# First feed-forward of a four-layer kernel: the last tile of the inner dimension stacked, gate on up and high part on low part

## What is computed

```
gate = einsum('bsh,oh->bso', x, lut[gate_idx])      # gate_idx, up_idx: 688 x 256
up   = einsum('bsh,oh->bso', x, lut[up_idx])
h    = silu(gate) * up                              # inner dimension 688
out  = einsum('bsh,oh->bso', h, lut[down_idx])      # down_idx: 256 x 688
```

## Time and profile before

| | |
|---|---|
| median of 3 runs | 2064.55 us (2063.49 to 2067.57) |
| profiled execution | 2068.32 us, span 2066.5 us |
| granted TensorE clock, mean of the span | 0.952 of full speed |
| PE busy | 1837.7 us, 89% of the span, 13335 instructions |
| PEld busy | 1266.3 us, 61% |
| DVE busy | 1374.8 us, 67%, 3587 instructions |
| ACT busy | 740.8 us, 36% |
| POOL busy | 901.9 us, 44%, 965 instructions |
| chain that ended last, by engine | PE 68%, DVE 19%, issue 6%, POOL 2%, ACT 2% |
| largest line of the chain | PE L1029, 16% |

### The profile page before, as it was taken

The page is one execution under the profiler, slowest core; times in us unless marked ns, Lnnn a source line. Parts: engine busy times, 40 slices in busy tenths (PEclk is TensorE's granted clock), DMA queues, the critical chain, the costliest instruction groups (busy, mean ns, idle before and its releaser), DMA issues.

```text
span 2066.5 us, 39950 instructions
## 1 busy us (share of the span) xinstructions
PE 1837.7 (89%) x13335; PEld 1266.3 (61%) x13400; DVE 1374.8 (67%) x3587; ACT 740.8 (36%) x1511; POOL 901.9 (44%) x965
## 2 busy tenths in 40 slices
PE   8999999689997899999999988899867788998887
PEld 5555555489996455555555446677655667885443
DVE  4677767465554656565656567888846776886775
ACT  2544444122222464656464541111122223443332
POOL 0354545465555254545454443333343224663333
PEclk9999999799999899999999999999999888999787
DMA  5300000100004646454545400000011000000011
GB/s 181 106 6 8 5 8 6 35 6 10 9 10 95 138 84 112 84 109 81 109 81 111 79 7 14 8 10 8 15 32 41 13 16 16 16 13 18 31 38 41
DMA packets 68177, 93.34 MB, mean 45 GB/s; under 512 B 9852, under 2 KB 62316, under 8 KB 64748
## 3 DMA queue, kind: packets, MB, share of 16 engines
q1 hardware_dynamic: 68076, 92.01, 19.6%
HBM read 61.70 MB, written 29.49 MB: 44 GB/s over the span
## 4 chain that ended last, share of the span: by engine, by line
PE 68%; DVE 19%; issue 6%; POOL 2%; ACT 2%; DMA 1%; DVEq 1%; SPq 0%; POOLq 0%; ACTq 0%
PE PS L1029 16%; PE PS L2084 3%; PE PS L677 3%; DVE negmax L2322 3%; PE PS L1960 3%; PE PS L1196 3%; PE PS L734 3%; PE PS L750 2%; PE PS L510 2%; PE PS L2012 2%; DVE xn L500 2%; PE PS L2015 2%; PE PS L731 2%; PE PS L2057 2%; PE PS L701 1%
## 5 line engine op out<-in xcount | busy, mean ns | idle before, releaser
L2322 DVE TENSOR_REDUCE negmax<-PS 128x2 f32<-128x512 f32 (+1 forms) x384 | 247.1, 685 | 191.6 <-PE PS L2015 98.0
L541 POOL TENSOR_TENSOR X<-X,y_sb 128x512 f32 (+1 forms) x128 | 165.2, 1291 | 147.7 <-DVE y_sb L536 142.7
L536 DVE TENSOR_TENSOR y_sb<-PS,ga_sb 128x512 f32<-128x512 f32 x96 | 66.2, 690 | 180.3 <-PE PS L1029 50.4
L1029 PE MATMUL PS<-we_hi,h_parts 128*128 128x512 f32 x512 | 177.7, 407 | 1.6 <-POOL h_parts L1478 1.5
L500 DVE TENSOR_SCALAR xn<-X,mv,rs 128x256 f32 (+1 forms) x256 | 155.6, 649 | 22.5 <-POOL rs L493 21.2
L520 ACT ACTIVATE hT<-PS,modT 128x256 f32<-128x256 f32 x256 | 130.0, 559 | 112.5 <-PE PS L510 111.6
L2237 ACT ACTIVATE pw<-PS 128x512 f32<-128x512 f32 x256 | 139.0, 600 | 75.0 <-PE PS L2060 75.0
L491 POOL TENSOR_TENSOR rs<-mv,eps 128x2 f32<-128x2 f32 x128 | 26.6, 208 | 293.4 <-DVE mv L484 293.2
L1029 PE MATMUL PS<-l_h_parts,lut_hi 128*128 128x256 f32 (+1 forms) x768 | 145.7, 291 | 6.7 <-POOL l_h_parts L1162 6.7
L1029 PEld LDWEIGHTS PS<-l_h_parts,lut_hi 128*128 128x128 f32 (+1 forms) x768 | 117.8, 184 | 9.7 <-issue 5.4
L1572 DVE SCALAR_TENSOR_TENSOR l_acc<-PS,rt_g,l_acc 128x256 f32<-128x256 f32 x256 | 105.8, 475 | 20.8 <-PE PS L1029 20.7
(11 more groups left out here) (279 smaller groups left out, 4372.3 us busy)
## 6 DMA issues: line engine op xcount, KB each, us to landing
ga_sb<-ga_dram SPq DMA_DIRECT2D x128, 128.0 KB, 2.9
qk_dram<-qk_parts SPq DMA_DIRECT2D x64, 192.0 KB, 2.8
KS<-qk_dram SPq DMA_DIRECT2D x32, 384.0 KB, 5.9
QS<-qk_dram SPq DMA_DIRECT2D x32, 384.0 KB, 9.3
qk_dram<-qk_parts SPq DMA_DIRECT2D x64, 128.0 KB, 2.8
wmod<-in_wmod SPq DMA_DIRECT2D x4, 1536.0 KB, 13.6
qk_dram<-qk_parts SPq DMA_DIRECT2D x64, 64.0 KB, 2.5
y_out<-X SPq DMA_DIRECT2D x16, 256.0 KB, 2.2
```

The source lines that it names most:

```text
L541: pool.tensor_tensor(xb(b), xb(b), y_sb[b.par][:, :, :], ALU.add).then_inc(s.x.sem, 1)
L1029: last_ = pe.matmul(out, x.bitcast(F32R), y.bitcast(F32R), start=start and n == 0, stop=stop and n == 2)
L2322: dve.tensor_reduce(to, src, AX.X, ALU.max, negate=True).then_inc(s.max.sem, 1)
```

## The change

The tiles of the inner dimension become 4 of 128, one of 112 and one of 64 (TAIL) rows. The index layout puts the last 64 columns of up directly behind gate, so that the last 64 columns of gate and of up are one weight tile of 128 columns: its product has gate on PSUM partitions 0 to 63 and up on 64 to 127. ACT writes the silu to partitions 64 to 127, DVE multiplies there and writes `hid` to partitions 0 to 63. The rows of the last tile of down stand twice, on partitions 0 to 63 and 64 to 127. The low part of the last hidden tile is made by DVE, no longer by POOL, and written to partitions 64 to 127 under the high part, so that one 128-row matmul gives high x high and low x high; a 64-row one gives high x low.

```
--- before.py
+++ after.py
@@ -27,6 +27,7 @@
 HD = D // HEADS
 INTER = 688
 FT = -(-INTER // P)
+TAIL = P // 2
 LUT = 16
 EPS_DEN = 1e-6
 LAMBDA_INIT = 0.8 - 0.6 * math.exp(-0.3 * 12)
@@ -160,10 +161,13 @@
     out["l0_side"] = (k[:, None] // HD % 2 == np.arange(2)[None, :]).astype(f)
     age = age[:, 0:P]
 
-    pad = np.zeros((FT * P - INTER, D), np.int32)
-    down = np.concatenate([a["L0_ffn_down_idx"].T, pad]).reshape(FT, P, D).transpose(1, 0, 2)
-    out["l0_idx"] = np.concatenate([two(a["L0_ffn_gate_idx"].T).reshape(P, -1), two(a["L0_ffn_up_idx"].T).reshape(P, -1),
-                                    down.reshape(P, -1)], 1)
+
+    tail = np.arange(INTER - TAIL, INTER)
+    order = np.concatenate([np.arange((FT - 1) * P) % INTER, tail, tail])
+    down = np.ascontiguousarray(a["L0_ffn_down_idx"].T)[order].reshape(FT, P, D).transpose(1, 0, 2)
+    up = a["L0_ffn_up_idx"].T
+    both = two(np.concatenate([a["L0_ffn_gate_idx"].T, up[:, INTER - TAIL:], up[:, 0:INTER - TAIL]], 1))
+    out["l0_idx"] = np.concatenate([both.reshape(P, -1), down.reshape(P, -1)], 1)
     out["l0_lut"] = a["L0_ffn_lut"]
 
     out["l2_b"] = two(a["L2_attn_B"].T)
@@ -1031,10 +1035,13 @@
 
 
 
-        gate_w = [w[:, 0:KH * INTER].rearrange("p (k n) -> p k n", k=KH) for w in (lut_hi, lut_lo)]
-        up_w = [w[:, KH * INTER:2 * KH * INTER].rearrange("p (k n) -> p k n", k=KH) for w in (lut_hi, lut_lo)]
+
+
+        both_w = [w[:, 0:2 * KH * INTER].rearrange("p (k n) -> p k n", k=KH) for w in (lut_hi, lut_lo)]
+        gate_w = [w[:, :, 0:INTER] for w in both_w]
+        up_w = [w[:, :, INTER + TAIL:2 * INTER] for w in both_w]
         down_w = [w[:, 2 * KH * INTER:].rearrange("p (m d) -> p m d", m=FT) for w in (lut_hi, lut_lo)]
-        rows_of = lambda m: min(P, INTER - m * P)
+        rows_of = lambda m: TAIL if m == FT - 1 else min(P, INTER - TAIL - m * P)
 
         def l0f_tensor(pe, pl, s):
             psum_free(pe, pl)
@@ -1049,10 +1056,15 @@
                             pe.wait_ge(*s.hid(i, m - 2))
                         elif (i - 1).ok:
                             pe.wait_ge(*s.hid(i - 1, m + 4))
-                        for n, w in enumerate((gate_w, up_w)):
+                        if m == FT - 1:
                             for kh in range(KH):
-                                last_ = matmul3(pe, PS[0:r, 1 + m % 3, n * T:(n + 1) * T], [x[:, kh, m * P:m * P + r] for x in w],
+                                last_ = matmul3(pe, PS[:, 1 + m % 3, 0:T], [x[:, kh, INTER - TAIL:INTER + TAIL] for x in both_w],
                                                 [l0_h_parts[i.par][:, c, kh, :] for c in range(2)], kh == 0, kh == 1)
+                        else:
+                            for n, w in enumerate((gate_w, up_w)):
+                                for kh in range(KH):
+                                    last_ = matmul3(pe, PS[0:r, 1 + m % 3, n * T:(n + 1) * T], [x[:, kh, m * P:m * P + r] for x in w],
+                                                    [l0_h_parts[i.par][:, c, kh, :] for c in range(2)], kh == 0, kh == 1)
                         if m == FT - 1:
                             last_.then_inc(s.hfree.sem, 1)
                         else:
@@ -1070,11 +1082,15 @@
                     if (b - 1).ok:
                         pe.wait_ge(*s.y(b - 1))
                     for t in range(TT):
-                        for m in range(FT):
+                        for m in range(FT - 1):
                             r = rows_of(m)
                             last_ = matmul3(pe, bank(4)[:, t * D:(t + 1) * D],
                                             [hid_parts[b.par][0:r, c, m, t * P:(t + 1) * P] for c in range(2)],
-                                            [x[0:r, m, :] for x in down_w], m == 0, m == FT - 1)
+                                            [x[0:r, m, :] for x in down_w], m == 0, False)
+
+                        for n, w in ((P, down_w[0]), (TAIL, down_w[1])):
+                            last_ = pe.matmul(bank(4)[:, t * D:(t + 1) * D], hid_parts[b.par][0:n, 0, FT - 1, t * P:(t + 1) * P].bitcast(F32R),
+                                              w[0:n, FT - 1, :].bitcast(F32R), start=False, stop=n == TAIL)
                     last_.then_inc(s.y_ps.sem, 1)
 
             slots(pe, slot, -1, (4, 14), B)
@@ -1098,7 +1114,8 @@
                             act.wait_ge(*s.hid(i, m - 2))
                         elif (i - 1).ok:
                             act.wait_ge(*s.hid(i - 1, m + 4))
-                        act.activation(act_sb[m % 3][0:r, :], PS[0:r, 1 + m % 3, 0:T], ACT.Silu).then_inc(s.gate.sem, 1)
+                        at = TAIL if m == FT - 1 else 0
+                        act.activation(act_sb[m % 3][at:at + r, :], PS[0:r, 1 + m % 3, 0:T], ACT.Silu).then_inc(s.gate.sem, 1)
                         if m == (1 if i.reg is None and i.off == B - 1 else 2):
                             ahead(modulate, act, pl, i, 1)
                         if i.reg is None and i.off == B - 1 and m in (3, 4):
@@ -1135,14 +1152,22 @@
                             dve.wait_ge(*s.hid_lo(i, m - 2))
                         elif (i - 1).ok:
                             dve.wait_ge(*s.hid_lo(i - 1, m + 4))
-                        dve.tensor_tensor(hid[m % 3][0:r, :], act_sb[m % 3][0:r, :], PS[0:r, 1 + m % 3, T:2 * T],
-                                          ALU.mult).then_inc(s.hid.sem, 1)
+                        if m == FT - 1:
+                            act_, up_ = act_sb[m % 3][TAIL:P, :], PS[TAIL:P, 1 + m % 3, 0:T]
+                        else:
+                            act_, up_ = act_sb[m % 3][0:r, :], PS[0:r, 1 + m % 3, T:2 * T]
+                        dve.tensor_tensor(hid[m % 3][0:r, :], act_, up_, ALU.mult).then_inc(s.hid.sem, 1)
                         if m == 0 and (i - 2).ok:
                             dve.wait_ge(*s.y_ps(i - 2))
                         if m == 0:
                             ahead(ln_apply, dve, pl, i, 1)
                         dve.wait_ge(*s.hid(i, m + 1))
                         split_hi(dve, hid_parts[i.par][0:r, 0, m, :], hid[m % 3][0:r, :]).then_inc(s.hid_hi.sem, 1)
+                        if m == FT - 1:
+                            dve.wait_ge(*s.hid_hi(i, FT))
+                            dve.wait_ge(*s.hid_lo(i, FT - 1))
+                            dve.tensor_tensor(hid_parts[i.par][TAIL:P, 0, m, :].bitcast(F32R), hid[m % 3][0:r, :],
+                                              hid_parts[i.par][0:r, 0, m, :], ALU.subtract).then_inc(s.hid_lo.sem, 1)
                         if m == 4 and (i + 1).ok:
                             high_bits(i + 1)
                         if m == 2 and i.reg is None and i.off == B - 1:
@@ -1167,9 +1192,10 @@
                 if i.ok:
                     for m in range(FT):
                         r = rows_of(m)
-                        pool.wait_ge(*s.hid_hi(i, m + 1))
-                        pool.tensor_tensor(hid_parts[i.par][0:r, 1, m, :].bitcast(F32R), hid[m % 3][0:r, :], hid_parts[i.par][0:r, 0, m, :],
-                                           ALU.subtract).then_inc(s.hid_lo.sem, 1)
+                        if m < FT - 1:
+                            pool.wait_ge(*s.hid_hi(i, m + 1))
+                            pool.tensor_tensor(hid_parts[i.par][0:r, 1, m, :].bitcast(F32R), hid[m % 3][0:r, :], hid_parts[i.par][0:r, 0, m, :],
+                                               ALU.subtract).then_inc(s.hid_lo.sem, 1)
                         if m == 4 and (i + 1).ok:
                             low_bits(i + 1)
                         if m >= 4 and i.reg is None and i.off == B - 1:
```

## The result

| | before | after |
|---|---|---|
| median | 2064.02 us (4 runs, 2063.12 to 2067.57) | 2053.54 us (4 runs, 2051.76 to 2059.82) |
| ratio, 95% interval | | 0.9947 (0.993 to 0.9964) |
| profiled execution, span | 2068.32, 2066.5 us | 2059.82, 2057.4 us |
| granted clock | 0.952 | 0.950 |
| PE busy, matmuls | 1837.7 us, 13335 | 1824.3 us, 13207 |

The kernel became faster by about 10.5 us where 13.7 were forecast: in the range, and short of the middle by a quarter. The counts are as the change says: 128 matmuls fewer, 16 instructions more on DVE, 16 fewer on POOL.

The account below looks back on a forecast made before the run. PE, busy 236.2 of 248.0 us in the layer, was taken as the bound. Slots 13.3 plus hand-over 0.4 gave 13.7 us, so 2064.55 - 13.7 = 2050.9 us; range 2045.5 to 2056.5.

Parts of the forecast that it names:

- The bound and the slots: PE full; slot i, gate/up of block i and down of block i-1, gains 0.95 us; slots 1 to 14 give 13.3.
- Parts 1 and 2: Last tile: gate and up lose six matmuls, 0.71 us a slot; down loses one per half, 0.24 us a slot.
- The step between row counts: Down product: each step between 128 and 48 rows costs about 0.19 us; four a slot remain, at the same price.
- Rivals B and C: B: 112-row steps cost too, 2061.5 us, chance 0.06. C: narrow weights cost drains, 5.3 us more gain, 2045.6, chance 0.02.
- The clock after the wait in slot 3: PE's lower clock after idling for DVE's rows: a quicker recovery could give back 0.8 us; not taken.
- Part 3: Last hidden tile's low-part subtraction moves from POOL to DVE: 0.4 to 1.2 us there, hidden by idle time, cost zero.
- Part 4: Hand-over in block 15: q's split on POOL earlier, the DMA queue's 0.43 us wait goes, QS earlier; bounds 0 and 0.72.
- Rival D: Slot tails: DVE and POOL block each other and become the bound; 10.5 us slower, 2075 us, chance 0.03.
- Rival E: Gain given back at the hand-over, where the attention's start hangs on something else; within 0.2%, chance 0.03.

Follow-up runs that it names:

- gate_only: Changed kernel with the last down tile again three 64-row matmuls per half and its low part on POOL: median 2055.9 us, ratio 0.9956 to before.
- full_rows: Changed kernel with the last down tile's second matmul over 128 rows instead of 64, adding low x low: median 2045.8 us, ratios 0.9901 and 0.9905 to before.
- sizes_only: Kernel before with tiles of 128, 112 and 64 rows, nothing stacked, low part on POOL: 2065.7 us in one execution, slots 13.97 us.
- before_padded: Kernel before plus two waits and a one-column memset per block of this phase in VectorE's program: median 2064.2 us, ratio 0.9996 to before.
- full_rows_nudged: full_rows with 16 one-column memsets more in VectorE's program at the end of the phase: median 2046.5 us, ratio 0.9908 to before.
- low_on_pool: Changed kernel with the last hidden tile's low part back on POOL, with waits for POOL's own work: median 2052.8 us, ratios 0.9951 and 0.9939 to before.
- full_rows_pool: full_rows with the last hidden tile's low part on POOL, no instruction added on VectorE: median 2042.4 us, ratios 0.9884 and 0.9902 to before.

## Why the prediction came out as it did

**The bound and the slots: right.** PE is full and every steady slot gives its matmuls back: 0.90 us for 0.95 forecast. Parts 1 and 2 are confirmed apart by gate_only, 0.70 for 0.71 and 0.20 for 0.24. The down product itself gave what was said: half of it takes 0.98 us where it took 1.10 (510.26 to 511.36), 0.24 a slot. The missing 0.05 us a slot lies among the gate and up matmuls, whose distances vary between 0.11 and 0.12 us in either kernel. The distances around the 64-row matmul add up as forecast (0.74 us for three) but do not lie as forecast: 0.21, 0.31 and 0.22, not 0.31 on either side. Slots 1 to 14 count, slot 0 does not (12.7 us from its transposes to the next, before and after).

**The step between row counts: right, and it was the larger prize.** 0.19 us a step was read from the earlier trace rows. full_rows measures 0.20. The prediction carried four steps a slot over as unavoidable; they were worth 10 us, nearly as much as the whole change. The Trainium skill (TensorEngine Tiling (Array Packing), Key Properties) has the drain at a change of mode; for the step to 48 or 64 rows the runs agree, for 112 rows (sizes_only) and for narrow weights (0.35 us a triple) there is none. Rivals B and C are out.

**The clock after the wait in slot 3: not taken, and rightly.** Slot 3's stretch from transposes to transposes was 16.87 us before and 15.27 after, 1.60 less where the others lose 0.9. That looks like 0.7 us given back by the clock (the prediction had left 0.8 as an unknown), but two kernels with the old slots have other values in the same place: 16.54 in sizes_only, and 15.56 in before_padded:

```profile
458.39 1.11 PE PS L510 x4
459.51 14.37 PE PS L1029 x108
473.95 0.66 PE PS L510 x4
```

After slot 3's wait the lower level (granted clock 0.50) lasts 5.9 us before, 2.9 in before_padded and 4.4 after. Over its own steady slot, slot 3 takes 2.9, 2.6 and 1.6 us more in the three profiles with the old slots and 2.2 to 2.4 in the three of the changed kernel. So the 0.7 us is a difference between two profiles, not shown to be one between the kernels.

**Part 3, the moved subtraction: the cost beside it was right, "cost zero" was not.** Beside the other work it was hidden: 0.42 us, with 1.46 us idle time behind it, slots equal on either engine. But the step priced an added instruction only by its duration and its waits. It also lengthens VectorE's program, and hundreds of microseconds later a stall of 0.30 us stands in the routing chain of the experts. With it the change pays 3.4 us in that phase (242.6 us for its 16 blocks, 239.2 before). That is the term that was mis-sized: 0 in the sum, +3.4 measured. Of 14 profiles, the seven without the added instructions show neither; the seven with them have the stall (in full_rows_nudged at an earlier step of the same block), and six of those the loss (3.3 to 3.8 us). It is shown that the stall goes with the added instructions (before_padded); that it comes from loading code is only argued. In those six profiles the lower level begins 0.9 to 1.3 us after PE's idle time ends and lasts 6.8 us. Why the clock falls there and not in before_padded stays open; one difference on record is that the stretches of low clock ahead of it stand at other distances (the last two ahead of the experts' blocks start 30.7 us apart in before_padded, 27.3 in the kernel before and in the changed one). The stall is needed for the loss but not enough for it: the six have the stall and an earlier start of the experts' phase, before_padded has the stall alone, gate_only, low_on_pool and full_rows_pool have the earlier start alone, and the loss came only with both. Whether it is the start itself that matters no run tells.

**Part 4, the hand-over: wrong.** The 0.43 us pause at 645.91 was read as a wait for POOL's split of q, behind k's six writes. Only five of them stand ahead of it; it lies between k's fifth and sixth, where nothing waits for POOL, and it is there unchanged when q is ready 0.7 us earlier. 0.4 forecast, 0 measured; the lower bound of that term held.

**The sum in its place.** 14 slots x 0.90 = 12.6 us, slot 3's clock 0, hand-over 0. The mean phases of three profiles each differ by 12.5 (245.4 and 232.9). Less 3.4 in the experts' phase: 9.1. Measured between means: 9.8, give or take 1.8. The same account, phase against means of all executions, holds for the others: gate_only 9.3 and 9.2; low_on_pool 12.4 and 12.2; full_rows 21.6 on average less 3.4 = 18.2, and 19.6; full_rows_pool 21.5 and 22.0. Each pair agrees within the interval of its means (about 2 us either way).
The time of the change was thus in the range because its main term was right and the loss that nobody expected was small beside it; that loss, not the parts 1 and 2, is why it lies at 2053.5 (2055.4 over 17 executions) and not at 2050.9.
Rival D did not come: POOL's long subtraction and DVE's conversion do block each other (1.50 us), once a slot, inside the slack. Rival E (given back at the hand-over) was right in kind and wrong in place: a quarter of the gain was given back, some 670 us after the phase that was changed.

## What to carry to other kernels

Where PE is full and streams short matmuls, price each by the distance of two starts, and look for pairs of starts that are further apart than the rest: a step from 128 rows to half of them and back cost 0.38 us around a single matmul here, as much as three matmuls of full height (0.36). If both operands can be filled to 128 rows with terms that do no harm, do it. And when an edit puts instructions on an engine, compare the later phases as well, block by block against the kernel before: the loss may be in code that nobody touched. Take no term from one pair of profiles where a third can be had: two profiles with the same slots differed by 1.3 us in a single slot here.

## What the runs showed that was not expected

- A phase that the change does not touch became about 3.4 us longer in all six profiles of kernels with the last low part on VectorE, and in none of the seven without instructions added there. The stall ahead of it is 0.30 us, less than a tenth of what followed.
- The same stall and the same 1.91 us of PE idle time left the clock at 1.00 in before_padded and were followed by the lower of the two levels (1.2 GHz) in the others.
- A conversion on VectorE stood for 1.50 us a slot (3.20 us in slot 0, with POOL's subtraction and a memset one after the other) where those of the first five tiles mostly take 0.29, and the two-input subtraction took 0.42 us behind it in steady slots but 1.22 us in block 15, while POOL was splitting k. The Trainium skill (SBUF — State Buffer, Who interferes with whom) has both cases, the conversion in its two-port mode and the operation with two SBUF inputs; these rows agree.
